# An FFT-convolution kernel: VectorE adds up the four products of two spectra, the inverse transform takes two operands, and a convolution chunk changes place

## The chip, the cores and the metric

The kernel runs on one core of one Trainium2 chip. The metric is the device time of one execution in microseconds (us); less is better. Engines: TensorE (PE in the profile: matrix products; PEld is its weight load), VectorE (DVE), ScalarE (ACT), GpSimd (POOL) and SyncE (SP), which issues the DMAs.

## The reference, cut to what matters

The input is 16 images of 32 channels and 128x128 pixels in fp32. A first stage normalizes each channel, applies a dynamic 3x3 depthwise convolution with a 1x1 convolution, and adds the input. The second stage, where the change lies, is this:

```python
hidden = einsum('oc,bchw->bohw', w_hidden, x)            # 32 -> 192 channels
hidden = depthwise_3x3(hidden, w_dw)
q, k, v = split(hidden, 3, axis=1)                       # 64 channels each
out = irfft2(rfft2(patches(q)) * rfft2(patches(k)))      # patches of 8x8 pixels
out_norm = (out - mean_c(out)) / sqrt(var_c(out) + 1e-5) * norm_w + norm_b
return einsum('oc,bchw->bohw', w_out, v * out_norm)      # 64 -> 32 channels
```

The product of the two spectra is complex: four real products for each frequency, of which two make the real part (kc*qc - ks*qs) and two the imaginary part (kc*qs + ks*qc). At frequencies that are their own mirror there is no sine part, and the kernel stores two of these real frequencies together, one in the place of the cosine, one in that of the sine.

## The kernel before, in words

After the first stage the second works through 32 units `u`, each half an image. A unit has two parts on each engine, `front(u, tail)` and `spectral(u, tail)`, where `tail` is the unit before. All orders are written out by hand, engines meet at semaphores, and each engine works strictly in its own order.

**Front.** VectorE copies 10x10 windows (`window`, L1102, eight rows of them for a unit, three buffers). TensorE makes 32 `hidden_group`s from them (L572) in a ring of three PSUM banks, and ScalarE copies each to `hwin` (L810). For the tail, VectorE works on eight pieces `p` of the inverse's result `Y`: `pixel_stats` (four statistics, L1112), `variance` (L1118, L1120), then GpSimd takes the root (L456), then `centre` (L1125) and `scale` (L1132). TensorE turns a scaled piece (`turn`, L600), ScalarE copies it with scale and shift (`turned_out`, L819), VectorE multiplies it with v (`gate`, L1137), TensorE projects (`project`, L609), VectorE adds the residual (`residual`, L1144). v comes from `v_chunk` (L587, 18 matmuls, nine taps), in eight chunks for a unit; `between` places hidden groups between the taps.

**Spectral.** Eight octets of channels `m`. `q_octet` (L647) and `k_octet` (L659) transform q and k, ScalarE copies q to SBUF (L852), and VectorE forms the four products in two instructions of 128x512 (L1197). `k_octet(m)` waits for the products of octet m-2. After every two octets an `inverse(e)` (L676) is due: four operand blocks (`both`) times four row groups times two column groups, 32 matmul calls or 64 instructions, that add up in PSUM:

```python
for both in range(4):
    for c in range(4):
        for lam in range(2):
            mm = pe.matmul(i_banks(e)[c][...], small["inverse"][32 * c:32 * c + 32, 64 * both:64 * both + 64],
                           at(prod[32 * c:32 * c + 32, :], 2048 * (e % 2) + 128 * both + 64 * lam, [512, 4], [1, 64]),
                           start=both == 0, stop=both == 3)
```

ScalarE copies each inverse to `Y` in four instructions (`inverse_out`, L865). Inverses 0 and 1 stand behind the octets 2 and 4; inverses 2 and 3 stand together behind octet 7, and `v_chunk(u, 0, 0, 0, None)`, the first chunk of v, follows them. TensorE's next work is three hidden groups, `v_chunk(tail, 0, 1, 5, hidden)` and `turn(tail, 0, 0)`, which waits for `scale(tail, 0)`. The first `pixel_stats` of a unit waits for all sixteen copies of its four inverses.

Of the kernel before, what the change touches and what calls it, by code (L numbers as in the profile page):

```python
# [25 lines left out]
TINY = 1e-30  # L26


TABLES = {"tables": (("identity", 128), ("inverse", 256), ("w_out", 64)),
          "weights": (("quarter_mean", 128), ("eye", 32), ("w1", 128), ("w2", 4), ("dyn_w", 36), ("conv1", 32),  # L30
                      ("conv1_b", 1), ("gamma", 1), ("beta", 1), ("hidden_qk", 32), ("dw_qk", 9), ("hidden_v", 32),
                      ("dw_v", 9), ("norm_w", 1), ("norm_b", 1))}
# [2 lines left out]
def constants():  # L35

    p = np.arange(128)
    same_channel = (p[:, None] % 32 == p[None, :] % 32).astype(np.float32)
    out = {"identity": np.eye(128, dtype=np.float32), "quarter_mean": same_channel / 4}
    out["eye"] = np.tile(np.eye(32, dtype=np.float32), (4, 1))  # L40

    u, v = np.divmod(np.arange(64), 8)
    mirror = 8 * (-u % 8) + -v % 8
    real = np.flatnonzero(mirror == np.arange(64))
    pairs = np.flatnonzero(mirror > np.arange(64))
    freq = np.concatenate([pairs, real[:2], pairs, real[2:]])
    sine = (np.arange(64) >= 32) & (np.arange(64) < 32 + len(pairs))
    angle = 2 * np.pi * ((u[freq][:, None] * u + v[freq][:, None] * v) % 8) / 8
    wave = np.where(sine[:, None], np.sin(angle), np.cos(angle)).reshape(64, 8, 8)
    spectra = np.zeros((9, 64, 10, 10), np.float64)  # L50
    for tap in range(9):
        dy, dx = tap // 3, tap % 3
        spectra[tap, :, dy:dy + 8, dx:dx + 8] = wave


    spectra = np.pad(spectra.reshape(9, 8, 8, 100), ((0, 0), (0, 0), (0, 0), (0, 28)))
    out["spectra"] = np.pad(spectra.transpose(2, 0, 1, 3).reshape(72, 8 * 128), ((0, 24), (0, 0))).astype(np.float32)
    row, tap = np.divmod(np.arange(72), 9)
    out["tap_rows"] = np.pad((tap == np.arange(9)[:, None]).astype(np.float32), ((0, 0), (0, 56)))
    out["row_mask"] = np.pad(np.repeat(row[:, None] == np.arange(8), 64, axis=1), ((0, 24), (0, 0))).astype(np.float32)  # L60
    cosines, sines = np.cos(angle), np.sin(angle)
    paired = np.arange(32)[:, None] < len(pairs)
    inverse = np.concatenate([np.where(paired, 2, 1) * cosines[:32], np.where(paired, 2 * sines[:32], 0), np.where(paired, 2 * sines[:32], 0),
                              np.where(paired, -2, 1) * cosines[32:]], axis=1) / 64
    out["inverse"] = np.tile(inverse, (4, 1)).astype(np.float32)
    return out


def build(nc, t, out):
# [22 lines left out]
    with ctx:  # L92
# [4 lines left out]
        def semaphore(name):  # L97
            return ctx.enter_context(nc.semaphore(name))
# [84 lines left out]
        s_q_copied = semaphore("q_copied")  # L183
        s_k_mm = semaphore("k_mm")
        s_prod_ready = semaphore("prod_ready")
        s_inverse_mm = semaphore("inverse_mm")
        s_y_ready = semaphore("y_ready")

# [14 lines left out]
        def at(ap, offset, *dims):  # L203

            return bass.AP(tensor=ap.tensor, offset=ap.offset + offset, ap=[ap.ap[0]] + [list(d) for d in dims])
# [258 lines left out]
        def _(pe):  # L464
# [147 lines left out]
            def front(u, tail):  # L612

                groups = iter(range(32 if u is not None else 0))

                def hidden(n=1):
                    for g in islice(groups, n):
                        hidden_group(u, g, banks[0:4] if tail is None else ring_banks)

                if tail is None:  # L620
                    hidden(8)
                    beside(NB, 5)
                    hidden(8)
                    beside(NB, 7)
                    hidden(16)
                    return
                hidden(3)
                for k in range(4):
                    v_chunk(tail, k, 1, (5, 5, 4, 3)[k], hidden)
                    if k > 0:  # L630
                        project(tail, k - 1)
                    turn(tail, k, 0)
                    if k < 3:
                        v_chunk(tail, k + 1, 0, (5, 4, 3)[k], hidden)
                    if k < 3 or u is None:
                        turn(tail, k, 1)

            def spectral(u, tail):
# [23 lines left out]
                    mm.then_inc(s_k_mm, 1)  # L662

                def inverse(e):
                    pe.wait_ge(s_prod_ready, 16 * u + 4 * e + 4)
                    if 0 < e < 3:
                        pe.wait_ge(s_y_ready, 16 * u + 4 * e)
                    if e == 0 and tail is not None:
                        pe.wait_ge(s_gated, 8 * u)
                        pe.wait_ge(s_t_copied, 8 * u)  # L670
                    if e == 3 and tail is not None:
                        pe.wait_ge(s_res_done, 4 * u)
                    for both in range(4):
                        for c in range(4):
                            for lam in range(2):
                                mm = pe.matmul(i_banks(e)[c][64 * lam:64 * lam + 64, 256 * (e % 2):256 * (e % 2) + 256],  # L676
                                               small["inverse"][32 * c:32 * c + 32, 64 * both:64 * both + 64],
                                               at(prod[32 * c:32 * c + 32, :], 2048 * (e % 2) + 128 * both + 64 * lam, [512, 4], [1, 64]),
                                               start=both == 0, stop=both == 3)
                    mm.then_inc(s_inverse_mm, 1)  # L680

                pe.wait_ge(s_h_ready, 32 * (u + 1))
# [3 lines left out]
                for m in range(8):  # L686
                    k_octet(m)
                    if m < 7:
                        q_octet(m + 1)
                    if m == 1 and tail is not None:  # L690
                        project(tail, 3)
                    if m in (2, 4):
                        inverse(m // 2 - 1)
                inverse(2)
                inverse(3)
                v_chunk(u, 0, 0, 0, None)

            front(0, None)
            spectral(0, None)
# [8 lines left out]
        def _(act):  # L708
# [138 lines left out]
            def spectral(u, tail):  # L847
                for m in range(8):
                    act.wait_ge(s_q_mm, 8 * u + m + 1)
                    if positive(16 * u + 2 * m - 2):  # L850
                        act.wait_ge(s_prod_ready, 16 * u + 2 * m - 2)
                    act.activation(q_sb[m % 2], q_bank, ACT.Copy).then_inc(s_q_copied, 1)  # L852
                    if m == 0 and tail is not None:
                        turned_out(tail, 3, 1)
                    if m in (3, 5):
                        inverse_out(u, m // 2 - 1)
                inverse_out(u, 2)
                inverse_out(u, 3)

            def inverse_out(u, e):  # L860
# [22 lines left out]
        def _(dve):  # L883
# [262 lines left out]
            def front(u, tail):  # L1146
                rows = iter(range(3, 8) if u is not None else ())

                def windows(n=1):
                    for r in islice(rows, n):  # L1150
                        window(u, r)

                if tail is None:
# [7 lines left out]
                    for i in range(4):  # L1161
                        low(NB - 1, i)
                    return
                for p in range(3):
                    pixel_stats(tail, p)
                    variance(tail, p)
                    if p == 1:
                        centre(tail, 0)
                windows()
                scale(tail, 0)  # L1170
                centre(tail, 1)
                scale(tail, 1)
                windows()
                for p in range(8):
# [10 lines left out]
                    if p in (2, 4, 6):  # L1185
                        residual(tail, p // 2 - 1)

            def spectral(u, tail):
                for n in range(16):
                    m, quad = n // 2, n % 2  # L1190
                    if quad == 0:
                        dve.wait_ge(s_q_copied, 8 * u + m + 1)
                        dve.wait_ge(s_k_mm, 8 * u + m + 1)
                        if positive(4 * u + m // 2 - 1):
                            dve.wait_ge(s_inverse_mm, 4 * u + m // 2 - 1)
                    first = 1024 * (m % 4) + 512 * quad
                    dve.tensor_tensor(prod[:, first:first + 512].rearrange("p (a b x) -> p a b x", a=2, b=2),  # L1197
                                      at(k_banks[m % 2], 256 * quad, [128, 2], [0, 2], [1, 128]),
                                      at(q_sb[m % 2], 256 * quad, [0, 2], [128, 2], [1, 128]), ALU.mult).then_inc(s_prod_ready, 1)
                    if n == 1 and tail is not None:  # L1200
                        gate(tail, 3, 1)
                    if n == 3 and tail is not None:
                        residual(tail, 3)
                    if u < LAST and n in (8, 10, 12):
                        window(u + 1, n // 2 - 4)

            dve.wait_ge(s_win_room, 3)
            for r in range(3):
# [50 lines left out]
```

## Time and profile before

| What | Value |
|---|---|
| Median of three executions | 2357.64 us (2355.62 to 2362.33) |
| The profiled execution, its own time | 2366.28 us |
| Its span, first to last instruction | 2364.4 us |
| Mean granted TensorE clock | 0.972 |
| Busy: PE, DVE, ACT, POOL | 95%, 68%, 62%, 21% |
| Second stage | from about 535 us to the end, 32 units |

The profile is of one execution. Busy shares are averages over stages that differ. The page lists groups of instructions by their line; the trace behind it can be read in order of time, by waits, and by stretches of the span. The end of a matmul is modelled, so where two groups follow each other on TensorE the difference of their starts says more than the busy time.

### The profile page before, as it was taken

What the parts mean: (1) busy time and instruction counts of PE and PEld (TensorE: products, weight loads), DVE (VectorE), ACT (ScalarE), POOL (GpSimd) and SP (SyncE); (2) the same over time, 40 slices, a digit from 0 to 9 for tenths busy, and PEclk for the clock granted to TensorE, in tenths of its full rate; (3) what the DMA queues carried; (4) which work ended last, traced back from release to release, by engine and by line L of the source; (5) the groups of instructions that cost most, each with busy time, mean ns of one, the idle gap of its engine ahead of it and who ended that gap; (6) DMA issues with size and microseconds to landing.
All of it is one profiled execution on the core that took longest, in us unless ns stands there. A gap on an engine that the chain in (4) does not pass through costs nothing.

```text
span 2364.4 us, 107028 instructions
## 1 busy us (share of the span) xinstructions
PE 2236.0 (95%) x48375; PEld 1443.6 (61%) x48375; DVE 1613.8 (68%) x4058; ACT 1454.2 (62%) x2629; POOL 486.3 (21%) x323
## 2 busy tenths in 40 slices
PE   7888888868999999999999999999999999999997
PEld 3333333346666666777676766667666666667664
DVE  5566766646777767767677667777777777777775
ACT  3456655566666666666666666666666666666662
POOL 1000000002222222222222222222222222222222
PEclk9889988978999999999999999999999999999999
DMA  7689888784333333333333333333333333333312
GB/s 140 168 212 234 226 204 219 214 200 103 75 76 76 76 76 76 79 81 76 84 73 79 76 84 80 84 81 84 76 84 76 83 78 76 76 76 76 76 43 50
DMA packets 60409, 248.63 MB, mean 105 GB/s; under 512 B 12393, under 2 KB 12658, under 8 KB 53810
## 3 DMA queue, kind: packets, MB, share of 16 engines
q1 hardware_dynamic: 59954, 241.78, 43.3%
q8 instruction: 381, 6.24, 1.1%
q14 instruction: 74, 0.61, 0.1%
HBM read 140.02 MB, written 101.72 MB: 102 GB/s over the span
## 4 chain that ended last, share of the span: by engine, by line
PE 84%; DVE 7%; ACT 4%; issue 4%; DMA 1%; SPq 0%; POOL 0%; POOLq 0%; ACTq 0%
PE bank L587 18%; PE bank L527 16%; PE bank L676 11%; PE bank L659 10%; PE bank L647 9%; PE bank L572 7%; PE bank L600 7%; PE bank L609 5%; DVE arena L1112 3%; ACT arena L865 2%; DVE arena L1132 1%; DVE arena L1125 1%; ACT arena L819 1%; DVE arena L1102 1%; ACT arena L724 1%
## 5 line engine op out<-in xcount | busy, mean ns | idle before, releaser
L456 POOL TENSOR_TENSOR arena<-arena 128x8 f32<-128x8 f32 x256 | 462.1, 1805 | 1357.6 <-DVE arena L1118 1352.6
L587 PE MATMUL bank<-arena 128*64 128x512 f16 x4608 | 689.9, 393 | 0.0
L810 ACT ACTIVATE arena<-bank 100x512 f32<-100x512 f32 x1024 | 606.6, 628 | 95.4 <-PE bank L572 75.1
L1197 DVE TENSOR_TENSOR arena<-bank,arena 128x512 f32<-128x512 f32 x512 | 337.2, 687 | 207.8 <-issue 174.0
L572 PEld LDWEIGHTS bank<-arena 128*36 128x36 f16 (+1 forms) x8192 | 330.5, 104 | 232.4 <-issue 23.5
L527 PE MATMUL bank<-arena 32*32 32x508 f32 (+1 forms) x9216 | 382.9, 649 | 55.4 <-issue 40.6
L572 PE MATMUL bank<-arena 128*36 128x128 f16 (+1 forms) x8192 | 390.5, 221 | 17.4 <-DVE arena L1102 11.5
L819 ACT ACTIVATE arena<-bank,arena 128x256 f32<-128x256 f32 x512 | 261.1, 560 | 119.9 <-PE bank L600 119.4
L852 ACT ACTIVATE arena<-bank 128x512 f32<-128x512 f32 x256 | 153.2, 598 | 265.7 <-PE bank L647 265.2
L1112 DVE BATCH_NORM_STATS2 arena<-arena 128x6 f32<-128x128 f32 x1024 | 221.7, 279 | 121.3 <-ACT arena L865 121.3
L647 PE MATMUL bank<-arena 100*32 100x128 f32 x8192 | 277.5, 274 | 5.2 <-issue 3.9
L659 PE MATMUL bank<-arena 100*32 100x128 f32 x8192 | 278.3, 274 | 0.7 <-issue 0.7
L1137 DVE TENSOR_TENSOR arena<-arena,bank 128x512 f32<-128x512 f32 x256 | 175.3, 685 | 145.9 <-ACT arena L819 145.8
L865 ACT ACTIVATE arena<-bank 128x256 f32<-128x256 f32 x512 | 155.3, 391 | 185.6 <-PE bank L676 185.6
L587 PEld LDWEIGHTS bank<-arena 128*64 128x64 f16 x4608 | 206.3, 109 | 96.0 <-ACT arena L865 10.5
L527 PEld LDWEIGHTS bank<-arena 32*32 32x32 f32 x9216 | 142.4, 107 | 194.9 <-issue 163.6
L659 PEld LDWEIGHTS bank<-arena 100*32 100x32 f32 x8192 | 222.0, 109 | 55.5 <-issue 26.4
L676 PE MATMUL bank<-arena 32*64 32x256 f32 x8192 | 255.6, 380 | 0.2
L647 PEld LDWEIGHTS bank<-arena 100*32 100x32 f32 x8192 | 220.4, 109 | 21.2 <-issue 5.0
L676 PEld LDWEIGHTS bank<-arena 32*64 32x64 f32 x8192 | 180.8, 129 | 50.3 <-issue 16.8
L600 PEld LDWEIGHTS bank<-arena 128*128 128x128 f32 x1024 | 133.7, 195 | 119.3 <-DVE arena L1132 88.7
L600 PE MATMUL bank<-arena 128*128 128x128 f32 x1024 | 181.4, 300 | 18.1 <-DVE arena L1132 10.9
(112 smaller groups left out, 1605.1 us busy)
## 6 DMA issues: line engine op xcount, KB each, us to landing
arena<-xn_d SPq DMA_DIRECT2D x128, 536.2 KB, 4.8
xn_d<-arena SPq DMA_DIRECT2D x130, 260.0 KB, 4.5
x_d<-arena SPq DMA_DIRECT2D x64, 512.0 KB, 8.3
arena<-x_d SPq DMA_DIRECT2D x128, 256.0 KB, 4.2
out<-arena SPq DMA_DIRECT2D x128, 256.0 KB, 2.7
arena<-x_in SPq DMA_DIRECT2D x32, 544.0 KB, 9.6
arena<-x_in SPq DMA_DIRECT2D x32, 528.0 KB, 9.4
arena<-spectra_in SPq DMA_DIRECT2D x1, 384.0 KB
```

The source lines that it names most:

```text
L456: pool.tensor_tensor(tiny["rstd"][:, slot], tiny["var_eps"][:, slot], powers, ALU.pow).then_inc(s_root, 1)
L527: mm = pe.matmul(at(psum_of(t, r)[32 * c:32 * c + 32, :], low, [W, 4], [1, high - low]), conv_w[b % 2][32 * r:32 * r + 32, 32 * tap:32 * t ...
L572: mm = pe.matmul(ring[g % len(ring)][low:high, 128 * i:128 * i + 128], w[:, first + low:first + high], hidden_w, start=True, stop=True)
L587: mm = pe.matmul(v_banks[chunk % 3][64 * s:64 * s + 64, :], v_w[:, 64 * tap:64 * tap + 64], at(xs[u % 3], row * WP + 32 * k + dx, [32 * WP ...
L600: tr = pe.transpose(t_bank[:, 128 * i:128 * i + 128], at(Y, 8 * k + 4 * jr + i, [32, 128]), ident)
L647: mm = pe.matmul(q_bank[32 * c:32 * c + 32, first:first + 128], G_q[0:WIN, 64 * ch + 32 * part:64 * ch + 32 * part + 32], hwin[0:WIN, 128 ...
L659: mm = pe.matmul(k_banks[m % 2][32 * c:32 * c + 32, first:first + 128], G_k[0:WIN, 64 * ch + 32 * part:64 * ch + 32 * part + 32], hwin[0:W ...
L676: mm = pe.matmul(i_banks(e)[c][64 * lam:64 * lam + 64, 256 * (e % 2):256 * (e % 2) + 256], small["inverse"][32 * c:32 * c + 32, 64 * both: ...
L810: act.activation(h_rows[0:WIN, :, first:first + 4], ring[g % len(ring)][0:WIN, :].rearrange("p (i c) -> p c i", i=4), ACT.Copy).then_inc(s ...
L819: ins = act.activation(at(gated[jr], 256 * lam, [32, 8], [8, 4], [1, 8]), at(banks[4], 64 * lam, [8, 8], [128, 4], [1, 8]), ACT.Identity, ...
L1112: ins = dve.bn_stats(T["pixel_stats"][:, first:first + 6], at(Y, 2048 * s + 4 * p + j, [32, 64], [1, 2]))
L1197: dve.tensor_tensor(prod[:, first:first + 512].rearrange("p (a b x) -> p a b x", a=2, b=2), at(k_banks[m % 2], 256 * quad, [128, 2], [0, 2 ...
```

## The change

The constant `inverse` becomes half as wide and a column of signs `cross_sign` joins it: -1 for the paired frequencies, +1 for the places that hold two real frequencies. The forward waves at these places now hold half the sum and half the difference of the two real ones, so that the same two sums serve there too. Behind the two product instructions of an octet VectorE executes two more on SBUF (`spectrum`), each 128 partitions by 256 elements: the real part with SCALAR_TENSOR_TENSOR, the imaginary part with TENSOR_TENSOR, both in place; the first waits for VectorE's own products. `inverse` waits for these sums and makes 16 matmul calls, 32 instructions.

The order changes at four places. Inverse 2 moves ahead of `k_octet(7)`, with ScalarE's copies of it. The first chunk of v stands between `k_octet(7)` and inverse 3. The three hidden groups ahead of `v_chunk(tail, 0, 1)` go into it (eight between its taps instead of five). On VectorE the three windows for the next unit move from among the products to behind the last of them, and the start of `front` has a new order.

```diff
+            def spectrum(u, m):
+                first = 1024 * (m % 4)
+                dve.wait_ge(s_prod_ready, 16 * u + 2 * m + 2)
+                dve.scalar_tensor_tensor(at(prod, first, [512, 2], [1, 128]), at(prod, first + 384, [512, 2], [1, 128]),
+                                         small["cross_sign"], at(prod, first, [512, 2], [1, 128]), ALU.mult, ALU.add)
+                dve.tensor_tensor(at(prod, first + 128, [512, 2], [1, 128]), at(prod, first + 128, [512, 2], [1, 128]),
+                                  at(prod, first + 256, [512, 2], [1, 128]), ALU.add).then_inc(s_spectrum, 1)
...
 (VectorE, spectral)
+                    if quad == 1:
+                        spectrum(u, m)
...
-                    if u < LAST and n in (8, 10, 12):
-                        window(u + 1, n // 2 - 4)
+                if u < LAST:
+                    for r in range(3):
+                        window(u + 1, r)
...
 (TensorE, inverse)
-                    pe.wait_ge(s_prod_ready, 16 * u + 4 * e + 4)
+                    pe.wait_ge(s_spectrum, 8 * u + 2 * e + 2)
...
-                    for both in range(4):
+                    for part in range(2):
...
 (TensorE, spectral)
-                    if m in (2, 4):
+                    if m in (2, 4, 6):
                         inverse(m // 2 - 1)
-                inverse(2)
+                v_chunk(u, 0, 0, 0, None)
                 inverse(3)
-                v_chunk(u, 0, 0, 0, None)
...
 (TensorE, front)
-                hidden(3)
                 for k in range(4):
-                    v_chunk(tail, k, 1, (5, 5, 4, 3)[k], hidden)
+                    v_chunk(tail, k, 1, (8, 5, 4, 3)[k], hidden)
...
 (ScalarE, spectral)
-                    if m in (3, 5):
+                    if m in (3, 5, 7):
                         inverse_out(u, m // 2 - 1)
-                inverse_out(u, 2)
...
 (VectorE, front)
-                for p in range(3):
-                    pixel_stats(tail, p)
-                    variance(tail, p)
-                    if p == 1:
-                        centre(tail, 0)
+                pixel_stats(tail, 0)
+                variance(tail, 0)
                 windows()
+                centre(tail, 0)
+                pixel_stats(tail, 1)
+                variance(tail, 1)
                 scale(tail, 0)
                 centre(tail, 1)
+                pixel_stats(tail, 2)
+                variance(tail, 2)
                 scale(tail, 1)
                 windows()
```

## Rows read from the trace of the kernel before

**Rows 1.** The page, busy time, share and instructions of each engine

```profile
PE 2236.0 (95%) x48375; PEld 1443.6 (61%) x48375; DVE 1613.8 (68%) x4058; ACT 1454.2 (62%) x2629; POOL 486.3 (21%) x323
```

**Rows 2.** Waits of TensorE: us in total, times, longest

```profile
PE bank L600 <- DVE arena L1132: 10.9, 32, 1.6
```

**Rows 3.** Busy time of a unit: stretch, length, engines, PEclk, DMA share, GB/s

```profile
1400.00:1456.18 56.18, 55.65 (x1228) 38.95 (x1220) 40.28 (x101) 36.48 (x72) 14.48 (x8) 1.00 0.36 80
```

**Rows 4.** TensorE in order of time, a unit's end: start, us, what

```profile
1453.70 1.08 PE L609 MATMUL bank<-arena 128*64 128x512 f32 x4
...
1460.29 1.06 PE L659 MATMUL bank<-arena 100*32 100x128 f32 x32
1461.19 1.08 PE L647 MATMUL bank<-arena 100*32 100x128 f32 x32
1462.21 2.00 PE L676 MATMUL bank<-arena 32*64 32x256 f32 x64
1464.14 1.08 PE L659 MATMUL bank<-arena 100*32 100x128 f32 x32
...
1468.94 3.74 PE L676 MATMUL bank<-arena 32*64 32x256 f32 x128
1472.61 2.26 PE L587 MATMUL bank<-arena 128*64 128x512 f16 x18
1474.70 0.83 PE L572 MATMUL bank<-arena 128*64 128x128 f16 x24
...
1479.05 0.71 PE L600 MATMUL bank<-arena 128*128 128x128 f32 x4 [0.33 <-DVE arena L1132]
...
1486.84 0.60 PE L609 MATMUL bank<-arena 128*64 128x512 f32 x2
```

**Rows 5.** VectorE in order of time, the same stretch

```profile
1451.22 1.29 DVE L1197 TENSOR_TENSOR arena<-bank,arena 128x512 f32<-128x512 f32 x2 [0.64 <-issue]
1452.43 0.68 DVE L1137 TENSOR_TENSOR arena<-arena,bank 128x512 f32<-128x512 f32 x1
...
1474.04 0.87 DVE L1112 BATCH_NORM_STATS2 arena<-arena 128x6 f32<-128x128 f32 x4 [3.62 <-ACT arena L865]
...
1475.10 0.87 DVE L1112 BATCH_NORM_STATS2 arena<-arena 128x6 f32<-128x128 f32 x4
...
1477.82 0.57 DVE L1102 COPY arena<-arena 128x1600 f16<-128x1600 f16 x1
1478.31 0.69 DVE L1132 TENSOR_TENSOR arena<-arena 128x512 f32<-128x512 f32 x1
1478.91 0.69 DVE L1125 TENSOR_TENSOR arena<-arena 128x512 f32<-128x512 f32 x1
1479.71 0.69 DVE L1132 TENSOR_TENSOR arena<-arena 128x512 f32<-128x512 f32 x1
...
1485.41 0.68 DVE L1137 TENSOR_TENSOR arena<-arena,bank 128x512 f32<-128x512 f32 x1
```

**Rows 6.** ScalarE in order of time, the same stretch

```profile
1472.79 1.21 ACT L865 ACTIVATE arena<-bank 128x256 f32<-128x256 f32 x4 [0.53 <-PE bank L676]
1475.13 4.29 ACT L810 ACTIVATE arena<-bank 100x512 f32<-100x512 f32 x8 [1.12 <-PE bank L572]
```

**Rows 7.** GpSimd in order of time, one unit earlier

```profile
1418.83 5.66 POOL L456 TENSOR_TENSOR arena<-arena 128x8 f32<-128x8 f32 x3 [32.90 <-DVE arena L1118]
```

**Rows 8.** VectorE by line and form: busy us, mean ns, idle before

```profile
L1118 DVE TENSOR_SCALAR arena<-arena 128x8 f32<-128x8 f32 x256 | 44.2, 173 | 8.8
...
L1049 DVE SCALAR_TENSOR_TENSOR arena<-arena 128x9 f32<-128x9 f32 x48 | 11.0, 228 | 1.7
```

**Rows 9.** Busy time of short stretches, columns as in rows 3

```profile
556.00:561.00 5.00, 2.10 (x70) 1.72 (x66) 3.08 (x6) 0.60 (x1) 0.00 (x0) 1.00 0.41 85
561.00:563.00 2.00, 2.00 (x46) 1.63 (x38) 0.00 (x0) 0.60 (x1) 0.00 (x0) 0.57 0.03 8
563.00:565.00 2.00, 2.00 (x51) 1.31 (x53) 1.29 (x2) 0.00 (x0) 0.00 (x0) 0.57 0.00 0
...
2320.00:2325.00 5.00, 3.83 (x34) 1.73 (x30) 4.03 (x20) 0.83 (x3) 2.83 (x2) 1.00 0.39 87
```

More of the change, by code:

```diff
@@ L26 @@
 TINY = 1e-30
-TABLES = {"tables": (("identity", 128), ("inverse", 256), ("w_out", 64)),
+TABLES = {"tables": (("identity", 128), ("inverse", 128), ("w_out", 64), ("cross_sign", 1)),
           "weights": (("quarter_mean", 128), ("eye", 32), ("w1", 128), ("w2", 4), ("dyn_w", 36), ("conv1", 32),
@@ L45, in constants @@
     pairs = np.flatnonzero(mirror > np.arange(64))
[L46 to L49, printed above, removed]
+    angle = 2 * np.pi * ((u[:, None] * u + v[:, None] * v) % 8) / 8
+    cosine, sine = np.cos(angle), np.sin(angle)
+    half_sum, half_diff = (cosine[real[:2]] + cosine[real[2:]]) / 2, (cosine[real[:2]] - cosine[real[2:]]) / 2
+    wave = np.concatenate([cosine[pairs], half_sum, sine[pairs], half_diff]).reshape(64, 8, 8)
     spectra = np.zeros((9, 64, 10, 10), np.float64)
@@ L60, in constants @@
     out["row_mask"] = np.pad(np.repeat(row[:, None] == np.arange(8), 64, axis=1), ((0, 24), (0, 0))).astype(np.float32)
[L61 to L65, printed above, removed]
+    inverse = np.concatenate([2 * cosine[pairs], 2 * half_sum, 2 * sine[pairs], 2 * half_diff]).reshape(2, 32, 64)
+    out["inverse"] = np.tile(np.concatenate([inverse[0], inverse[1]], axis=1) / 64, (4, 1)).astype(np.float32)
+    out["cross_sign"] = np.tile(np.where(np.arange(32) < len(pairs), -1, 1)[:, None], (4, 1)).astype(np.float32)
     return out
@@ L185, in build @@
         s_prod_ready = semaphore("prod_ready")
+        s_spectrum = semaphore("spectrum")
         s_inverse_mm = semaphore("inverse_mm")
@@ L676, in inverse @@
                                 mm = pe.matmul(i_banks(e)[c][64 * lam:64 * lam + 64, 256 * (e % 2):256 * (e % 2) + 256],
-                                               small["inverse"][32 * c:32 * c + 32, 64 * both:64 * both + 64],
-                                               at(prod[32 * c:32 * c + 32, :], 2048 * (e % 2) + 128 * both + 64 * lam, [512, 4], [1, 64]),
-                                               start=both == 0, stop=both == 3)
+                                               small["inverse"][32 * c:32 * c + 32, 64 * part:64 * part + 64],
+                                               at(prod[32 * c:32 * c + 32, :], 2048 * (e % 2) + 128 * part + 64 * lam, [512, 4], [1, 64]),
+                                               start=part == 0, stop=part == 1)
                     mm.then_inc(s_inverse_mm, 1)
```

## The prediction

> **What bounds the kernel now.** I read the page first: TensorE is busy 95% of the span, no other engine over 68% [rows 1]. A share of the whole span says little of one place, so I took the second stage unit by unit. One unit is 56.18 us long, TensorE works 55.65 of them at the full granted clock, VectorE 40.28, ScalarE 36.48 [rows 3]. So every unit is set by TensorE's own order of work, but for small gaps. The list of waits names the regular one: the first turn of a piece waits for its scaling on VectorE, 10.9 us in 32 waits, 0.34 for each [rows 2]. VectorE has 16 us of room in a unit; the question is where in the unit the room lies. For that I read one unit's end in order of time, engine by engine [rows 4 to 6].
>
> Two marks in it carry the sum. V is the start of what follows the last octet of k: 1468.94, where inverses 2 and 3 begin. T is the start of the first turn: 1479.05 [rows 4]. From V to T pass 10.11 us: two inverses 3.67, the chunk of v 2.09, then 4.35 for three groups, a chunk and five groups, of which 0.33 is the wait.
>
> **TensorE's part.** Inverses 2 and 3 together take 1472.61 - 1468.94 = 3.67, so 64 instructions cost 1.84 [rows 4]. Between octets one takes 1.93 to the next start, and the octet ahead of it 1.02 where the one before took 0.90, so each change of kind costs some 0.1 on either side. The change drops half of the instructions of each inverse: -0.92 each, on the path wherever TensorE isn't waiting. The changes of kind stay for inverses 0 and 1: V comes 2 x 0.92 = 1.84 earlier through them. Inverse 2 now stands ahead of V: 1.93 + 0.10 - 0.92 = +1.11. New V: 1468.94 - 1.84 + 1.11 = 1468.21. Bounds of the halving: 0.92 if the time goes with the instructions, 0.7 if part of it is fixed; I take the first, as the double run costs twice the single one.
>
> **VectorE's part, octets.** A 128x512 operation lasts 0.69 and the next starts 0.60 after it; 512 operands account for 0.53 at one element in 1.04 ns, which leaves 0.07 fixed [rows 5]. The operands are two of SBUF or one of PSUM, with no difference. So the plain sum of 256 elements has a pitch of 0.33 and a duration of 0.42. A wait for an operation of VectorE itself raises the pitch: scale behind centre 0.80 instead of 0.60 [rows 5], so +0.19 for `spectrum`'s wait. The real part is a form that the trace has only at nine columns: 228 ns, against 173 for one of eight columns without a pointer operand [rows 8]. I add these 0.06: pitch 0.39. Bounds: 0.33, as the plain sum, and 0.66, if it takes as long as a 512-column operation. I take 0.39, since the nearest rows show a surcharge and no slope. An octet then costs 0.60 + 0.79 + 0.39 + 0.33 = 2.11 us of VectorE, 1.20 before.
>
> Does it keep up? The first products start at 1451.22 [rows 5]; eight octets and the gate and the residual among them (0.60 each) would be through at 1451.22 + 16.88 + 1.20 = 1469.30 if it never waited. V is 1468.21, and the last products start some 0.2 after V. 0.2 + 2.11 after V is 1470.52, later than 1469.30, so the start of octet 7 sets it, not backlog. Early on VectorE falls back by 0.6 us behind the gate and residual; octet 3 stands behind an inverse and makes it good. The gate comes 0.9 later, ends at 1453.98, and the projection at 1453.70 needs it only for its second half, 0.45 later: no stall. `k_octet(m)` waits for octet m-2, a full 1.8 us or more behind. These are hidden by that room; without it each 0.1 costs 0.1. The windows come behind the last sum, three times 0.49 [rows 5], and end at about 1472.0; the statistics start at 1473.1, so they cost nothing, and the first group that needs one starts no earlier than 1472.3.
>
> **From V to T after.** (a) Inverse 3 waits for the sums of octet 7: 0.20 + 0.60 + 0.79 + 0.39 + 0.42 and 0.05 for the signal, 2.45 after V. The chunk of v covers 2.09, a stall of 0.36. (b) Inverse 3 takes 0.92 + 0.10, ScalarE starts 0.18 after the last start (1472.79 against 1472.61, rows 6), and its four copies take 1.25 until VectorE starts (1474.04): 2.45. (c) VectorE: statistics and variance 1.06 (1475.10 - 1474.04), window 0.48, centre 0.60, statistics and variance 1.06, scale 0.69 and 0.05 to TensorE, 3.94 [rows 5]. Before it was 5.01. The root isn't later: it takes 1.9 [rows 7], begins 0.3 behind the variance and is there 3.1 after the start, scale starts at 3.20. So T = V + 2.45 + 2.45 + 3.94 = 1477.05, where it was 1479.05: **2.0 us a unit**. Counted from the start of inverse 3, T stands at 6.39, and TensorE has 1.02 + 4.02 = 5.04 us of work there. ScalarE starts on the hidden groups at 2.42, behind the inverse's copies, and copies one each 0.52 (eight in 4.29, rows 6); the last of eight groups needs the fifth copy, at 5.02, and TensorE is through at about 5.5. So ScalarE spreads its work out but doesn't set T; TensorE then waits 0.9 for the scaling. Window 3 in (c) needs group 3, done at about 3.5, and is due at 3.51; here I expect up to 0.1 more.
>
> Half of the matmul saving is thus lost. Of 3.68 us, 0.33 of old wait is won as well; lost are 0.36 in (a), some 1.4 between inverse 3 and T, 0.3 for changes of kind.
>
> **Behind T.** Window 4 and all behind it come 0.85 later on VectorE, as one statistics piece moved behind T. The gate that the projection needs ends at 1486.09, the projection starts at 1486.84, its second half 0.45 later [rows 4, 5]: 0.75 + 0.45 of room. No cost. SP's queue: the residual's load waits for inverse 2, which comes earlier; the store of the unit before it waits for residual 3, about 1 us later, with over 10 us until use. No DMA is added.
>
> **Sum.** 31 units with a front behind them, 2.0 each, and 2.3 in the last (no windows or groups there): 64 us. The first stage isn't touched. The profiled execution took 2366.3 us (span 2364.4, 2 around it) and would become 2302; it was 8.6 above the median of the runs. Applied to the median, 2357.6 - 64 = **2294 us**.
>
> **Rivals.** (1) All waits hidden: the chain of (b) and (c) runs behind TensorE's work. V to T is then 2.09 + 1.02 + 4.02 = 7.13 and the unit gains 3.7, 119 us in all: 2239. For it speaks TensorE's 95%; against it that the chain would have to be 1.7 shorter, and its rows are of this place.
>
> (2) The real part at the pitch of a 512-column operation, 0.66. An octet is 2.38, VectorE never waits: 1451.22 + 19.04 + 1.20 = 1471.46, 0.1 more to the end of the sum and 0.05 to inverse 3, T at 1478.0 and the unit gains 0.75: 24 us, 2334. Nine columns [rows 8] can't exclude it; that plain two-operand operations of SBUF run at the full rate speaks against it. The Trainium skill, "Vector Engine (DVE) Microarchitecture Reference", section 7 ("Points that are easy to get wrong"), says this form with two non-bf16 operands in SBUF halves the throughput; by that rule 2334 is the time, and no row here decides it.
>
> (3) Slower: VectorE becomes the bound of the spectral part. With both new operations at 0.60, the first also with its 0.06, an octet is 2.65: 1451.22 + 21.20 + 1.20, and T is at 1480.2, 1.2 to 1.4 later than before, some 42 us: 2400. It turns at an octet of 2.47 us. Against it: 256 elements would have to cost what 512 do.
>
> (4) The new waits let TensorE's clock fall. Where TensorE was busy 2.10 of 5 us at the first unit, the next 4 us show 0.57, the 1.2 GHz level for most of them [rows 9]; that costs some 1.7 us, and once a unit would leave 0.3 of the 2.0: 2348. With 3.83 of 5 busy in the last unit the clock stayed at 1.00, and V to T after has about 7 of 8.8. The Trainium skill, "TensorE: Matmul & The Clock Gate" ("HAM oscillation"), tells of such a fall from short idles between groups of matmuls; the trace agrees for the first case alone.
>
> **Numbers.** My forecast 0.72, own range 2276 to 2314 (pitch 0.33 and no cost for the new change of kind, or 0.7 for the halving and a dependent wait of 0.3); (1) 0.06; (2) 0.11; (3) 0.06; (4) 0.05. The range reaches half-way to (1) and over (2): 2262 to 2338. 0.3%, 7 us, is about what can be told from no change. Faster 0.90, same 0.04, slower 0.06.
>
> **What would show it.** L676 half as many and near 128 us busy; SCALAR_TENSOR_TENSOR at 0.45 to 0.50 us (0.75 is rival 2); inverse 3 waiting 0.3 to 0.5 on VectorE; the first turn waiting about 0.8 on L1132 (in its new line); a unit of 54.2 us; PE's share down to 93%; the clock at 1.00. Wrong it would be if VectorE has no idle time between octets 3 and 7, or if a wait appears at the gates behind T.

## The result and the profile after

The changed kernel takes 2345.97 us, the kernel before 2361.32 in the same comparison (medians of 14 runs each); the ratio is 0.9938, 95% interval 0.9923 to 0.9953. It is 15 us faster, where 64 were forecast. The profiled execution after spans 2352.2 us. Below, medians and ratios leave out slow executions: one of e3's six took 2950 us at a granted clock of 0.653, where the others show 0.97.

The page of the changed kernel, busy time of each engine, and its costliest groups where they differ from before or should (line, engine, operation, forms and count | busy us, mean ns | idle before):

```profile
PE 2192.9 (93%) x44279; PEld 1343.9 (57%) x44279; DVE 1869.5 (79%) x4570; ACT 1527.0 (65%) x2629; POOL 501.7 (21%) x323
...
L807 ACT ACTIVATE arena<-bank 100x512 f32<-100x512 f32 x1024 | 692.4, 761 | 26.5 <-PE bank L571 23.8
...
L1108 DVE BATCH_NORM_STATS2 arena<-arena 128x6 f32<-128x128 f32 x1024 | 265.5, 322 | 37.3 <-ACT arena L861 37.3
...
L1133 DVE TENSOR_TENSOR arena<-arena,bank 128x512 f32<-128x512 f32 x256 | 175.0, 683 | 102.6 <-ACT arena L816 102.6
...
L1128 DVE TENSOR_TENSOR arena<-arena 128x512 f32<-128x512 f32 x256 | 189.9, 742 | 21.0 <-POOL arena L455 1.2
L1121 DVE TENSOR_TENSOR arena<-arena 128x512 f32<-128x512 f32 x256 | 186.6, 729 | 0.0
```

The copies to `hwin` and the statistics on the page of before:

```profile
L810 ACT ACTIVATE arena<-bank 100x512 f32<-100x512 f32 x1024 | 606.6, 628 | 95.4 <-PE bank L572 75.1
...
L1112 DVE BATCH_NORM_STATS2 arena<-arena 128x6 f32<-128x128 f32 x1024 | 221.7, 279 | 121.3 <-ACT arena L865 121.3
```

VectorE is busy 255.7 us more than before [rows 1]. The sums explain 232 of it (256 times 486 and 420 ns, below). Besides them, instructions that the change doesn't touch became slower. The copies to `hwin` took 628 ns and take 761 (ScalarE, the same 1024 of the same form), the statistics 279 and 322, scale 694 and 742, centre 686 and 729. The statistics alone are busy 43.8 us more; busy times of neighbours overlap, so the groups don't add up to the total. The gate, of the same size as scale, did not change: 685 and 683.

VectorE by line and form, the new operations:

```profile
L1190 DVE SCALAR_TENSOR_TENSOR arena<-arena 128x256 f32<-128x256 f32 x256 | 124.4, 486 | 9.1
L1192 DVE TENSOR_TENSOR arena<-arena 128x256 f32<-128x256 f32 x256 | 107.4, 420 | 0.0
```

TensorE in order of time from the last octets to behind the first turn (start, us, what), to be read against [rows 4]:

```profile
1404.34 1.13 PE L674 MATMUL bank<-arena 32*64 32x256 f32 x32
1405.40 1.08 PE L657 MATMUL bank<-arena 100*32 100x128 f32 x32
1406.41 2.26 PE L586 MATMUL bank<-arena 128*64 128x512 f16 x18
1408.80 1.13 PE L674 MATMUL bank<-arena 32*64 32x256 f32 x32
...
1415.66 0.71 PE L599 MATMUL bank<-arena 128*128 128x128 f32 x4 [0.95 <-DVE arena L1128]
...
1423.65 1.66 PE L608 MATMUL bank<-arena 128*64 128x512 f32 x4
1425.24 0.71 PE L599 MATMUL bank<-arena 128*128 128x128 f32 x4
...
1447.62 1.39 PE L608 MATMUL bank<-arena 128*64 128x512 f32 x4
1448.94 1.08 PE L657 MATMUL bank<-arena 100*32 100x128 f32 x32
```

V is 1406.41, T is 1415.66: 9.25 us where 8.84 were forecast. Inverse 3 starts 2.39 behind V (forecast 2.45). The first projection lasts 1.59 to the next start instead of 0.96, the one in the spectral part 1.32 instead of 1.01. Both wait for a gate, and a wait at the gates behind T is what the prediction named as a sign of being wrong.

VectorE in order of time, from the last sums to the first scaling, against [rows 5], and ScalarE's copies of the first eight groups, against [rows 6]:

```profile
1406.60 1.29 DVE L1204 TENSOR_TENSOR arena<-bank,arena 128x512 f32<-128x512 f32 x2 [0.55 <-issue]
1407.93 0.48 DVE L1190 SCALAR_TENSOR_TENSOR arena<-arena 128x256 f32<-128x256 f32 x1
1408.33 0.42 DVE L1192 TENSOR_TENSOR arena<-arena 128x256 f32<-128x256 f32 x1
1408.66 1.54 DVE L1098 COPY arena<-arena 128x1600 f16<-128x1600 f16 x3
1411.29 1.06 DVE L1108 BATCH_NORM_STATS2 arena<-arena 128x6 f32<-128x128 f32 x4 [1.08 <-ACT arena L861]
```

```profile
1411.11 4.92 ACT L807 ACTIVATE arena<-bank 100x512 f32<-100x512 f32 x8
```

The four statistics take 1.06 where they took 0.87 [rows 5], eight copies 4.92 where they took 4.29 [rows 6]. A unit, busy time of a stretch from one first turn to the next:

```profile
1415.66:1471.65 55.99, 54.51 (x1089) 36.02 (x1089) 48.27 (x117) 38.77 (x73) 14.95 (x9) 1.00 0.37 85
```

It is 55.99 us against 56.18 [rows 3] and the 54.2 of the forecast; the clock is the full one. The unit of rows 3 is one of the shorter ones: from first turn to first turn the 31 stretches of the kernel before last 56.50 on average, those of the changed kernel 56.06.

The last unit is different. It has no hidden groups, so TensorE waits 3.51 us for the first scaling. The granted clock behind it is 0.50, and the first chunk of v behind the turn takes 3.40 us to the next start:

```profile
2312.47 1.03 PE L599 MATMUL bank<-arena 128*128 128x128 f32 x4 [3.51 <-DVE arena L1128]
2313.43 3.48 PE L586 MATMUL bank<-arena 128*64 128x512 f16 x18
```

### The profile page after: what moved, and what is told of

Same layout as the page of the kernel before. It is cut to its first block, busy times and chain, and to the rows that moved or that the text cites. A ratio compares the mean times of both kernels' runs of the same rounds, so it can differ in the third digit from the quotient of the medians.

```text
span 2352.2 us, 99348 instructions
## 1 busy us (share of the span) xinstructions
PE 2192.9 (93%) x44279; PEld 1343.9 (57%) x44279; DVE 1869.5 (79%) x4570; ACT 1527.0 (65%) x2629; POOL 501.7 (21%) x323
## 4 chain that ended last, share of the span: by engine, by line
PE 75%; DVE 14%; issue 5%; ACT 4%; DMA 1%; POOL 0%; SPq 0%; ACTq 0%; POOLq 0%
PE bank L526 16%; PE bank L586 15%; PE bank L657 10%; PE bank L645 9%; PE bank L608 6%; PE bank L674 6%; PE bank L571 6%; PE bank L599 5%; DVE arena L1108 5%; DVE arena L1204 2%; DVE arena L1128 2%; DVE arena L1121 2%; ACT arena L861 2%; DVE arena L1098 1%; ACT arena L816 1%
## 5 line engine op out<-in xcount | busy, mean ns | idle before, releaser
L455 POOL TENSOR_TENSOR arena<-arena 128x8 f32<-128x8 f32 x256 | 477.5, 1865 | 1330.2 <-DVE arena L1114 1330.0
L586 PE MATMUL bank<-arena 128*64 128x512 f16 x4608 | 710.2, 395 | 3.9 <-DVE arena L1133 0.2
L807 ACT ACTIVATE arena<-bank 100x512 f32<-100x512 f32 x1024 | 692.4, 761 | 26.5 <-PE bank L571 23.8
L571 PEld LDWEIGHTS bank<-arena 128*36 128x36 f16 (+1 forms) x8192 | 324.1, 104 | 255.7 <-ACT arena L807 32.7
L571 PE MATMUL bank<-arena 128*36 128x128 f16 (+1 forms) x8192 | 405.6, 221 | 19.0 <-DVE arena L1098 11.5
L1204 DVE TENSOR_TENSOR arena<-bank,arena 128x512 f32<-128x512 f32 x512 | 329.0, 684 | 77.2 <-issue 76.5
L1108 DVE BATCH_NORM_STATS2 arena<-arena 128x6 f32<-128x128 f32 x1024 | 265.5, 322 | 37.3 <-ACT arena L861 37.3
L586 PEld LDWEIGHTS bank<-arena 128*64 128x64 f16 x4608 | 213.0, 109 | 109.6 <-issue 15.2
L1128 DVE TENSOR_TENSOR arena<-arena 128x512 f32<-128x512 f32 x256 | 189.9, 742 | 21.0 <-POOL arena L455 1.2
L1121 DVE TENSOR_TENSOR arena<-arena 128x512 f32<-128x512 f32 x256 | 186.6, 729 | 0.0
```

What stands on the lines that cost most here:

```text
L455: pool.tensor_tensor(tiny["rstd"][:, slot], tiny["var_eps"][:, slot], powers, ALU.pow).then_inc(s_root, 1)
L571: mm = pe.matmul(ring[g % len(ring)][low:high, 128 * i:128 * i + 128], w[:, first + low:first + high], hidden_w, start=True, stop=True)
L586: mm = pe.matmul(v_banks[chunk % 3][64 * s:64 * s + 64, :], v_w[:, 64 * tap:64 * tap + 64], at(xs[u % 3], row * WP + 32 * k + dx, [32 * WP ...
L807: act.activation(h_rows[0:WIN, :, first:first + 4], ring[g % len(ring)][0:WIN, :].rearrange("p (i c) -> p c i", i=4), ACT.Copy).then_inc(s ...
L1108: ins = dve.bn_stats(T["pixel_stats"][:, first:first + 6], at(Y, 2048 * s + 4 * p + j, [32, 64], [1, 2]))
L1128: dve.tensor_tensor(piece, piece, over(T["rstd"][:, slot]), ALU.mult).then_inc(s_y_norm, 1)
```

## The experiments

A run is a stretch of neighbouring words, and a word has four bytes. The slower instructions have one thing in common: they read or write SBUF in many short runs. The statistics read `Y` in runs of two words; centre, scale and the copies to `hwin` have runs of four. The sixteen copies that fill the tables `G_q` and `G_k` ahead of the second stage write runs of eight, and they slowed too, from 596 to 656 ns:

```profile
L769 ACT ACTIVATE arena<-bank 128x512 f32<-128x512 f32 x16 | 9.0, 596 | 15.8 <-PE bank L541 15.8
```

```profile
L766 ACT ACTIVATE arena<-bank 128x512 f32<-128x512 f32 x16 | 9.9, 656 | 15.5 <-PE bank L540 15.5
```

The gate and the products write one run of 512 words each and kept their times; the inverse's copies, with eight runs of 32 words, went from 391 to 394 ns. The new tables have 321 words in a partition, the old ones 448, and every later buffer moved with them: `hwin` starts at word 875 instead of 1002, and `Y` stands a multiple of 1024 words behind it. Theory L says that the start of short runs costs, here at an odd word; theory C says that the instructions are slowed by what now runs beside them.

**Only the layout.** One line behind the tables in either kernel; the unused words are touched by nothing.

```diff
             packs = {"tables": take_tables("tables")}
             ident = small["identity"]
+            layout_pad = take(127)      # e1; 5 in e3, 1 in e10, 2 in e11; kernel before: 1 in e2, 6 in e4
```

> The changed kernel with 127 unused words behind the tables, so that every later buffer stands where it stood in the kernel before (the big buffers start at word 1002, not 875). Theory L (layout): the copies to hwin fall back to a mean of 628 ns, the statistics to 279, centre and scale to 686 and 694; V to the first turn 8.84 us, no wait of 0.6 at the first projection; a unit 54.3 us; 2300 us in all (2290 to 2308). Rival C (contention): these instructions are slower because VectorE and ScalarE now run beside other work; they stay at 761, 322, 729 and 742 ns and the time stays at 2346 (2339 to 2353).

> The kernel before with one unused word behind the tables; the big buffers start at word 1003, an odd one, as in the changed kernel (875). Order and work are as before. Theory L: hwin copies 761 ns, statistics 322, centre and scale 729 and 742; the three statistics and one centre ahead of the first turn cost 3 x 0.17 + 0.05 us more, gates behind it slip too, a unit is 0.6 to 1.5 us longer: 2380 to 2410 us. Rival C: nothing changes, 2361 (2354 to 2368).

> The changed kernel with 5 unused words, big buffers from word 880, a multiple of 16. Theory L: at least as fast as with base 1002 (2290 to 2305); if the price hangs on where runs of two and four words start, the copies to hwin (runs of four words) get faster still, below 628 ns, and the statistics (runs of two) stay at 279. Rival C: 2346.

> The kernel before with 6 unused words, big buffers from word 1008, a multiple of 16. Theory L: the copies to hwin get faster than 628 ns, but TensorE sets the unit, so 2355 to 2362 us. Rival C: 2361, with copies of 628 ns.

> The changed kernel with one unused word behind the tables: big buffers from word 876, a multiple of four but not of sixteen. If the price hangs on an odd first word alone, all four groups are as fast as in e3 (copies near 612 ns, statistics 278) and the time is 2312 us (2305 to 2318). If it hangs on a multiple of 16 words or on the distance moved, it lies between 2320 and 2346.

> The changed kernel with two unused words: big buffers from word 877, odd, one more than a multiple of four, where 875 and 1003 were three more. If any odd word costs, the statistics (runs of two words) take 322 ns and the copies (runs of four) some 750 again: 2346 us (2338 to 2352). If only three more than a multiple of four costs, it is 2312.

| Kernel | first word | median us | ratio to before | copy to hwin, statistics, scale (mean ns) |
|---|---|---|---|---|
| changed (as given) | 875 | 2345.97 | 0.9938 (0.9923 to 0.9953) | 761, 322, 742 |
| e11 | 877 | 2345.48 | 0.9938 (0.9915 to 0.9961) | 760, 322, 735 |
| e1 | 1002 | 2311.74 | 0.9788 (0.9762 to 0.9814) | 649, 278, 693 |
| e10 | 876 | 2312.05 | 0.9796 (0.9762 to 0.9831) | 612, 277, 690 |
| e3 | 880 | 2314.07 | 0.9785 (0.9758 to 0.9812) | 612, 277, 691 |
| e2, kernel before | 1003 | 2383.49 | 1.0085 (1.0054 to 1.0115) | 751, 322, 737 |
| e4, kernel before | 1008 | 2359.2 | 0.9997 (0.9976 to 1.0017) | 599, 280, 692 |

Theory C fell as the cause of the lost time. The same work in the same order is 34 us faster with 127 unused words, and one unused word is enough (e10); the kernel before, whose engines do nothing new, shows the slower copies, statistics and scalings and loses about 20 us when it is moved by one word (e2). Here the expectation was too high, 2380 to 2410 with 2395 in its middle; the median is 2383.49. Any odd word costs (875, 877, 1003), not the distance moved and not missing a multiple of 16 (876, 1002). The copies of four-word runs tell even starts apart too: 649 ns at 1002, 612 at a multiple of four. That is worth nothing here; e3 and e10 are no faster than e1. e1 and e3 also missed their ranges, 2290 to 2308 and 2290 to 2305: the padding gave back less than the whole shortfall, and the rest is looked for below.

A small share of theory C stays for the copies. From the same first word 1002 they take 628 ns in the kernel before and 630 in e6 (sums, old order), but 649 in e1 and e7 (new order with and without sums). So the new order costs them some 20 ns; why was not tested. The output of the statistics moved by 127 words as well, but those of the first stage, which read runs of 512 words and write the same six, kept their times (677 and 678 ns at L947 and L943).

The groups behind it, in the changed kernel at base 1002 (e1):

```profile
L808 ACT ACTIVATE arena<-bank 100x512 f32<-100x512 f32 x1024 | 606.3, 649 | 56.5 <-PE bank L572 38.6
...
L1109 DVE BATCH_NORM_STATS2 arena<-arena 128x6 f32<-128x128 f32 x1024 | 221.8, 278 | 37.3 <-ACT arena L862 37.3
```

and in the kernel before, one word further (e2):

```profile
L811 ACT ACTIVATE arena<-bank 100x512 f32<-100x512 f32 x1024 | 685.3, 751 | 62.7 <-PE bank L573 61.0
...
L1113 DVE BATCH_NORM_STATS2 arena<-arena 128x6 f32<-128x128 f32 x1024 | 264.5, 322 | 122.6 <-ACT arena L866 122.6
```

The times overlap less than means tell: the shortest copy at an odd word is 708 ns (changed kernel) where the median at 1002 is 637. So the shortest moved too, and not only those that meet other work.

TensorE in e1, with the old places restored:

```profile
1443.05 1.13 PE L675 MATMUL bank<-arena 32*64 32x256 f32 x32
1444.11 1.08 PE L658 MATMUL bank<-arena 100*32 100x128 f32 x32
1445.12 2.25 PE L587 MATMUL bank<-arena 128*64 128x512 f16 x18
1447.52 1.13 PE L675 MATMUL bank<-arena 32*64 32x256 f32 x32
...
1453.95 0.71 PE L600 MATMUL bank<-arena 128*128 128x128 f32 x4 [0.96 <-DVE arena L1129]
```

V to T is 1453.95 - 1445.12 = 8.83, the 8.84 of the forecast. e1 gains 50 us of the 64; by the medians it lacks 18 to 2294, as the kernel before is at 2361 in this comparison and was at 2358 in the forecast. Its unit is 54.90 long instead of 54.2: an inverse takes 1.06 to the next start, not 1.01 (three ahead of V, 0.15); the first projection 1.17 instead of 0.96; the projection in the spectral part 1.33 instead of 1.01.

**The gate ahead of the sums.** TensorE in e1 and then in e5, the projection in the spectral part and the octet behind it:

```profile
1430.36 1.39 PE L609 MATMUL bank<-arena 128*64 128x512 f32 x4
1431.69 1.08 PE L658 MATMUL bank<-arena 100*32 100x128 f32 x32
```

```profile
1415.18 1.08 PE L609 MATMUL bank<-arena 128*64 128x512 f32 x4
1416.19 1.08 PE L658 MATMUL bank<-arena 100*32 100x128 f32 x32
```

```diff
+                    if n == 1 and tail is not None:
+                        gate(tail, 3, 1)
                     if quad == 1:
                         spectrum(u, m)
-                    if n == 1 and tail is not None:
-                        gate(tail, 3, 1)
```

> Base 1002 as in e1, and the gate of the piece (3,1) stands ahead of the two sums of octet 0 on VectorE, not behind them. Theory W (a wait counts for the weight load too, so the gate that ends 0.2 us before the projection's second half would start still costs 0.3): the projection takes 1.0 us again instead of 1.33, a unit 0.3 us less than e1, 2302 us (2296 to 2308). Rival: the projection's 0.3 come from elsewhere, time as e1, 2312.

It takes 2300.84 us, ratio 0.9744 (0.9719 to 0.9769), and the projection 1.01 again.

By the count of the prediction the gate ends 0.2 us before the projection's second half. The single instructions show that this count was wrong. `project` makes two calls, one for each half of its output partitions, and each has two instructions. In e1 the gate ends at 1430.63, and the second call's loads and its first matmul start at 1430.68:

```profile
1429.95 0.68 DVE L1134 TENSOR_TENSOR arena<-arena,bank 128x512 f32<-128x512 f32 x1
1430.68 0.19 PEld L609 LDWEIGHTS bank<-arena 128*64 128x64 f32 x2
```

In e5 the gate is early, ends at 1414.58, and the two calls run side by side: all four loads lie within 0.20 us, and 0.2 us behind the projection's start two matmuls are under way (rows of the stretches 1430.58 to 1430.82 above and 1415.15 to 1415.40 here, the gates from VectorE's own order).

```profile
1413.90 0.68 DVE L1134 TENSOR_TENSOR arena<-arena,bank 128x512 f32<-128x512 f32 x1
1415.17 0.20 PEld L609 LDWEIGHTS bank<-arena 128*64 128x64 f32 x4 [0.20 <-issue]
1415.18 0.65 PE L609 MATMUL bank<-arena 128*64 128x512 f32 x2
```

So the second call is due 0.01 us behind the first, not 0.45; what comes at 0.45 to 0.48 is the second instruction of each call. In e1 the second call starts 0.32 late, and that is the whole price.

**Both gates behind T as well.**

```diff
                 for p in range(8):
+                    if p < 2:
+                        gate(tail, p // 2, p % 2)
                     if p < 5:
                         pixel_stats(tail, p + 3)
                         variance(tail, p + 3)
                     if p > 0:
                         windows()
-                    if p < 7 or u is None:
+                    if 1 < p < 7 or p == 7 and u is None:
                         gate(tail, p // 2, p % 2)
```

> As e5, and behind the first turn the gates (0,0) and (0,1) stand ahead of the statistics of pieces 3 and 4 on VectorE, not behind them. Theory W: the first projection takes 0.96 us again in place of 1.17, another 0.2 a unit less than e5: 2294 us (2289 to 2300), the time forecast for the change. Rival: the statistics, now later, hold up a later scaling or a window, and it is 2301 or more.

This is added to e5's edit. It takes 2295.61 us, ratio 0.9728 (0.9693 to 0.9764), and is the best version. Its first projection is short again:

```profile
1440.96 1.03 PE L609 MATMUL bank<-arena 128*64 128x512 f32 x4
1441.92 0.71 PE L600 MATMUL bank<-arena 128*128 128x128 f32 x4
```

**The two halves of the change alone.** e6 has the sums and the halved inverse in the old order (base 1002); e7 has the new order on all engines, with four operand blocks and no sums. The edit of e6 against the changed kernel, besides the padding, is the order's part of the diff taken back:

```diff
-                    if m in (2, 4, 6):
+                    if m in (2, 4):
                         inverse(m // 2 - 1)
-                v_chunk(u, 0, 0, 0, None)
+                inverse(2)
                 inverse(3)
+                v_chunk(u, 0, 0, 0, None)
...
+                    if u < LAST and n in (8, 10, 12):
+                        window(u + 1, n // 2 - 4)
```

> Base 1002, sums on VectorE and inverses of two operands, but the order of the kernel before on all engines (inverses 2 and 3 behind octet 7, v's first chunk behind them, windows among the products, the old start of front). My steps give: the windows push the sums of octet 7 to some 4 us behind V, TensorE idles 3 us between inverses 2 and 3, T 1.5 us later than in e1, 0.2 back at the first projection: 2350 us (2335 to 2365). Rival: VectorE's room hides the sums in the old order too, 2312 or less.

> The kernel before with the new order on all engines, but four operand blocks and no sums on VectorE. My steps give: inverse 3 full length behind v's chunk, V to T 9.4 us and 2.0 more ahead of V, 11.4 in place of 10.1, 0.2 at the first projection: a unit 1.5 us longer, 2405 us (2385 to 2415). Rival: the order is good by itself (less waiting for the turn), 2340 to 2361.

e7 takes 2408.02 us, ratio 1.0201 (1.0172 to 1.0231), as expected. e6 takes 2365.72, ratio 1.0017 (0.9999 to 1.0034), 16 more than the 2350 expected. TensorE in e6, inverses 2 and 3 and the chunk of v:

```profile
1404.81 1.13 PE L676 MATMUL bank<-arena 32*64 32x256 f32 x32
1408.74 1.28 PE L676 MATMUL bank<-arena 32*64 32x256 f32 x32 [2.80 <-DVE arena L1194]
1409.95 3.66 PE L587 MATMUL bank<-arena 128*64 128x512 f16 x18
```

and its granted clock in stretches (the third number from the end):

```profile
1405.00:1410.00 5.00, 2.20 (x66) 1.04 (x58) 3.61 (x8) 1.21 (x4) 0.00 (x0) 0.96 0.38 107
...
1410.00:1412.00 2.00, 2.00 (x12) 0.83 (x12) 0.69 (x4) 1.21 (x4) 0.00 (x0) 0.50 0.01 2
```

The wait of 2.80 us was foreseen; that the clock falls to the 1.2 GHz level behind it was not. The chunk of v takes 3.66 instead of 2.25 us. But the fall doesn't follow from the wait alone: of 31 such waits, most of them of 2.80 us, ten left the chunk its length. This is the unit behind the one above:

```profile
1465.96 1.13 PE L676 MATMUL bank<-arena 32*64 32x256 f32 x32 [2.80 <-DVE arena L1194]
1467.02 2.25 PE L587 MATMUL bank<-arena 128*64 128x512 f16 x18
```

In the 21 others the chunk is 0.5 to 1.5 us longer, 24 us in all, which is more than the 16 that the expectation missed. The Trainium skill, "TensorE: Matmul & The Clock Gate" ("HAM oscillation"), says that idling between groups brings the throttle back; the trace agrees for 21 of 31 units of e6 and for the last unit of the changed kernel (3.51 us). In the changed kernel's other units behind the first, which wait 0.95 us at the first turn, the granted clock stays at 1.00.

So neither half gains: alone they give +3 us (not told from none, and with the clock's 24 in it) and +46, together -49 at the same base. The new order puts the chunk of v into the time that the sums need, and without sums that chunk only delays inverse 3.

**Without the sums.**

```diff
-                    if quad == 1:
-                        spectrum(u, m)
...
-                    pe.wait_ge(s_spectrum, 8 * u + 2 * e + 2)
+                    pe.wait_ge(s_prod_ready, 16 * u + 4 * e + 4)
```

> Base 1002 and the new order, the inverse of two operands waits for the products; the two sums are left out, so the inverse works on two of the four products and the output isn't the reference's. It gives what the sums cost TensorE. My steps: inverse 3 starts right behind v's chunk (0.35 less) and the projection (3,1) doesn't wait (0.3 less): 0.65 a unit, 2291 us (2284 to 2300). If VectorE's work costs through contention for memory as well, instructions at the same places get shorter and it is below 2284.

e8 leaves out the sums and so computes something else; it only prices them. It takes 2297.5 us, ratio 0.9728 (0.9704 to 0.9752), 14 less than e1; the projection takes 1.01 and inverse 3 starts 2.19 behind V instead of 2.40. The sums' 232 us on VectorE thus cost TensorE 14 of e1's time. I had expected 21: the chunk of v and the change of kind behind it cover 2.19, not 2.09. Of the 0.53 us by which e8's units are shorter (54.39 against 54.92, medians from first turn to first turn), 0.32 are the projection's wait, which e5 removes with the sums in place.

## Why the prediction was wrong

**The step that failed** is (c) of the part from V to T, and the terms like it behind T: "statistics and variance 1.06", "centre 0.60" and the gates 0.85 later were taken from rows of before for instructions that the diff doesn't touch. They hold only at their old addresses. I read `"inverse", 128` and `"cross_sign", 1` as table sizes and not as a shift of every buffer behind them by 127 words. What it cost is measured: 2345.97 - 2311.74 = 34 us, of the 64 - 15 = 49 us by which the gain fell short. In a unit it is 55.99 - 54.90 = 1.09: 0.42 from V to T, and behind T 0.42 at the first projection and 0.20 at the chunk of v ahead of it, which both wait for gates that slip with the statistics. ScalarE's copies became slower too, but no wait of TensorE in this sum is put down to them, and from 649 to 612 ns (e1 to e10) nothing was gained.

**A second step failed by less**: "needs it only for its second half, 0.45 later: no stall" for the gate (3,1), and "0.75 + 0.45 of room. No cost" for the one behind T. The 0.45 isn't there, as the two calls start together. Without it the second gate has 0.75 of room by its rows and comes 0.85 later, and the first ends 0.27 behind the projection's start. They cost 0.32 and 0.21 a unit in e1; e5 and e9 give back 11 and 5 us by moving the gates alone.

**Mis-sized, but right in kind:** the halving saves 0.87 for each inverse between octets (1.93 to 1.06), not 0.92, 0.15 a unit; the inverse's line is busy 145.5 us in all, where 128 were given. With all three, 54.18 + 0.32 + 0.21 + 0.15 = 54.86, and e1 measures 54.90 in the unit shown. This closes one unit and not the whole: over 31 units the three terms make 21 us, and e1 lacks only 14. The forecast was made from a unit of 56.18, and the mean of before is 56.50, that of e1 55.00.

**Right:** V to T was forecast at 8.84 and is 8.83 in e1; its parts are 2.40, 2.48 and 3.95, where 2.45, 2.45 and 3.94 were given. The first is shorter as `spectrum`'s wait adds 0.12 to the pitch and not 0.19: it starts 0.72 behind the second products. The real part takes 486 ns where 0.45 to 0.50 us were given, and has a pitch of 0.40 (forecast 0.39). Against the rule of the Trainium skill's "Vector Engine (DVE) Microarchitecture Reference", section 7, which halves this form's throughput with two non-bf16 operands in SBUF, the measurement decides: 486 ns for 256 fp32 elements is 66 more than the plain sum of the same size, near the 55 that the nine-column rows showed [rows 8], and rival 2 is out. Its price was also added up wrongly: T at 1478.0 is 1.05 us ahead of 1479.05, not 0.75, which makes 2324 and not 2334; rival 3's 1480.2 is 1.15 later, some 37 us and not 42. Rival 3 is out, since VectorE idles 0.55 us ahead of the last products, and as much behind each earlier inverse. Rival 1 couldn't occur: TensorE waits 0.95 at the first turn, as counted. Rival 4 occurred once, in the last unit, for some 1.5 us; that its 2348 lies next to the measured 2346 is chance. The order of work was judged rightly: e7's 2408 was computed as 2405 before it ran. The forecast's 2294 itself is reached by e9, with the padding and three gates moved.

## What to carry to other kernels

When a table or a buffer changes size in a memory that is handed out word by word, write down the first word of every later buffer before and after; if one that is accessed in many runs of two, four or eight fp32 words goes from even to odd, its instructions get slower, and one word of padding put it right here (e10). In a profile the sign is that an untouched line of the same count and form has another mean, in its shortest instances too. Two edits that only pay together (cheaper inverse, a place to hide its operands' sums) have to be costed together. And where two matmul calls stand behind each other in the program, look at their single starts before you count on the time between them: here the second was due 0.01 us behind the first, and its start 0.32 us later cost 0.32.

## What the runs showed of the hardware that was not expected

- VectorE's and ScalarE's time hangs on where short runs start. Statistics that read 64 runs of two fp32 words: 277 to 280 ns from an even first word, 322 from an odd one, 0.7 ns a run. Copies that write 128 runs of four words: 599 to 612 ns from a multiple of four, 628 to 650 from 1002, 751 to 761 from an odd word, up to 1.2 ns a run. Scaling with 128 runs of four, read and written: 690 to 695 and 735 to 742. Copies that write 64 runs of eight: 596 to 599 and 655 to 656 (sixteen of them in each kernel), 0.9 ns a run. Copies that write eight runs of 32: 389 to 391 and 394 to 396. Gates, with one run of 512: 683 to 686 everywhere. Runs that straddle a boundary of 8 bytes would fit odd against even, but not the copies' 649 against 612, both from even words; the runs here varied only the first word, and the inside of the memory was not measured.
- The Trainium skill, "SBUF — State Buffer", section "Operand start alignment", asks of an fp32 operand's start only that it is a multiple of four bytes, says that this is about legality and not speed, and that its runs timed nothing; e2 shows that a start that is legal can cost time.
- The projection's two matmul calls, which write partitions 0 to 63 and 64 to 127, start 0.01 us apart when both operands are there (e5); the second starts 0.05 us behind its gate when it is late (e1).
- Behind an idle piece of 2.80 us, with TensorE busy 2.20 of 5 us, the granted clock fell to the 1.2 GHz level for some 2 us or more (e6), at a cost of 1.4 us in the chunk of v alone. The same idle piece at the same place, one unit later, left the chunk at its full-clock length; over the run it is 21 falls in 31 waits.
